# A two-part transformer block on one core: norms as two VectorE steps each, weight pieces split amid the masks, another opening

## The chip, the core and the metric

The kernel runs on one core of a Trainium2 chip. It is written engine by engine: TensorE (PE, with its weight loads PEld), VectorE (DVE), ScalarE (ACT), GpSimd (POOL) and the DMA queue of SyncE (SP) each run their own list of instructions in order, and wait for one another by semaphores. The metric is the device time of one execution in microseconds, the median of several runs.

## The reference

A modulation is computed from a small vector, then `x` (2 sequences of 2048 rows, 256 columns) goes through a stack of three linear-attention layers, gated and added to `x`, and then through two layers of local attention, gated and added again. The first stack, the "first half", is what the change touches.

```python
mod = (_silu(L0_c) @ L0_wmod).reshape(L0_c.shape[0], 6, 1, -1)
sa, ca, ga, sb, cb, gb = (mod[:, 0], mod[:, 1], mod[:, 2], mod[:, 3], mod[:, 4], mod[:, 5])
ga = (2 * (ga >= 0) - 1) * jnp.maximum(jnp.abs(ga), 0.25)
h = _layernorm(x, axis=-1) * (1 + ca) + sa
x = x + ga * _L0_attn_ref(h, ...)          # three layers, below
h = _layernorm(x, axis=-1) * (1 + cb) + sb
x = x + gb * _L0_ffn_ref(h, ...)           # two layers of local attention and an MLP
...
for l in range(L):                         # L = 3, 16 heads of 16
    q = (out @ Wq[l] + bq[l]).reshape(B, S, N_HEAD, dh)
    ...
    Qf = favor(q, omega[l])
    Kf = favor(k, omega[l])
    a = causal_linear_attention(Qf, Kf, v).reshape(B, S, D)
    a = a @ Wo[l] + bo[l]
    h = layer_norm(out + a, ln1_g[l], ln1_b[l])
    y = jax.nn.relu(h @ W1[l] + bf1[l]) @ W2[l] + bf2[l]
    out = layer_norm(h + y, ln2_g[l], ln2_b[l])
```

## The kernel before

The first half works in chunks of 512 rows (four tiles of 128): 8 chunks per layer, 24 in all. Every engine runs the same loop over `n`. Iteration `n` does the attention of chunk `n`, the output projection and first norm of chunk `w = n-1`, the MLP of chunk `m = n-2` (eight blocks `hb`: `up` on PE, `relu` on ACT, `rounded` on DVE, `down` on PE), and the second norm of chunk `z = n-3`. Operands of large products are split into a high half (`XTH`, `WH`, `RH`) and a low half (`XTL`, `WL`, `RL`), with three products for each; the low half is a subtraction, on DVE or on POOL. The order of an engine's work is written out by hand in the loops, so whatever stands behind a waiting instruction on its engine waits too.

PE in iteration `n`: `up` 0, `spread` (of the inverse denominators, tile `SPR`), `up` 1, `proj`, `down` 0, `proj`, `up` 2, `values`, `down` 1, `favor`, `up` 3, `favor`, `down` 2 (which needs RL of block 2 from POOL), `attn_out`, `key_sums` (needs ZC from POOL), `up` 4, `turn_k`, `down` 3, then four stages of `scores`, `up`, `down`, `sums`, where `sums` needs the masked scores U from DVE (`masks`); `down` 4 needs RL from POOL. In stage 3 the turned tiles of the next `proj` are made (`turn_x`), and DVE makes their low halves (`lower`, XTL).

A norm before is `statistics` on DVE, `rsqrt` on POOL, `normed` on DVE (line 1080, subtract the mean and multiply), then gain and bias on POOL: `gain1` and `bias1` for the first norm (1580, 1586), `second_norm` for the second (1605 to 1614; in the last layer also the gate and the sum with `x`, held in `PX`), `modulated` for the norm behind the stack (1622, 1624; chunks 16 to 23, `CH3`), `prologue` for the one ahead of it (1544, 1546; chunks 0 to 7, two iterations ahead of use). DVE's residual add `Z<-PS,X` (1240) waits for `second_norm` of two chunks earlier, whose tile it overwrites.

Weights come in 12 pieces per layer through two staging buffers `SG1`, so a piece may be loaded only when the piece before the last has been split. Pieces of layer 0 are all split ahead of the loop; those of layers 1 and 2 in iterations 7 to 10 and 15 to 18, three to five at a time behind the last masks or at the head of an iteration.

The opening loads constants and the modulation's weights (`wmod`, six DMAs), PE waits for all constants (`ZT` is the last) and makes 12 products into banks 0 to 5, DVE copies them, norms chunk 0 and computes the gates. The second half begins on every engine behind `first_half_over`.

## Time and profile before

| | us |
|---|---|
| median of 3 runs | 3425.41 (3416.5 to 3429.06) |
| profiled execution | 3431.8, of which span 3429.9 |
| busy PE / DVE / POOL / ACT | 2835.1 / 2123.1 / 1921.7 / 1441.5 |
| granted clock, mean | 0.918 |
| first half ends (last X) | about 1756 |

The page gives busy time by engine; windows cut it by stage; the list of waits says which engine's work ended another's idle time, and the timeline shows the instructions in order, each with the idle time before it in brackets. PE's two clock levels are 2.4 and 1.2 GHz; a granted clock of 0.96 over a stretch means that 8% of it ran at the lower level.

### The profile page before, as it was taken

How to read it: one execution, taken by the hardware profiler on the slowest of the kernel's cores; microseconds unless marked ns; L12 is line 12 of the kernel's file. 1: busy time of each engine (PE TensorE's matmuls, PEld its weight loads, DVE VectorE, ACT ScalarE, POOL GpSimd, SP SyncE). 2: the span in 40 equal slices, each digit the busy share in tenths (PEclk: the TensorE clock that was granted, in tenths of full speed). 3: DMA queues.
4: the chain of work that ended last, by engine and by line, in shares of the span. 5: the costliest groups of instructions: out<-in, count | busy, mean ns of one | idle time of the engine just before them, and what ended most of it. 6: DMA issues, size and time to landing. Idle time of an engine off the chain costs nothing. (4 is left out here: it accounts for less than half of the span.)

```text
span 3429.9 us, 61913 instructions
## 1 busy us (share of the span) xinstructions
PE 2835.1 (83%) x22184; PEld 2294.2 (67%) x22184; DVE 2123.1 (62%) x4931; ACT 1441.5 (42%) x3009; POOL 1921.7 (56%) x1732
## 2 busy tenths in 40 slices
PE   3698898989998988787627888898888889888886
PEld 1476776777776776676515677777667677767675
DVE  4556666665666665555435667666666766666664
ACT  1344344344353343333104554555545455545451
POOL 2356555555555556666655556555656655665653
PEclk7899999999999999999858899999999899999998
DMA  3000000010000010000020000000010100000000
GB/s 84 13 13 7 14 1 13 7 31 1 2 3 12 11 27 13 19 14 19 19 73 12 11 13 11 13 14 11 8 38 19 34 23 18 25 14 26 23 23 30
DMA packets 78001, 65.66 MB, mean 19 GB/s; under 512 B 15410, under 2 KB 72714, under 8 KB 77706
## 3 DMA queue, kind: packets, MB, share of 16 engines
q1 hardware_dynamic: 77706, 61.70, 6.1%
q8 instruction: 188, 3.08, 0.4%
q14 instruction: 107, 0.88, 0.1%
HBM read 49.10 MB, written 12.58 MB: 18 GB/s over the span
## 5 line engine op out<-in xcount | busy, mean ns | idle before, releaser
L967 ACT ACTIVATE PR<-PS,SM 128x256 f32<-128x256 f32 (+1 forms) x512 | 279.4, 554 | 444.3 <-DVE SM L1340 441.0
L858 ACT ACTIVATE FB<-PS,BC 128x512 f32<-128x512 f32 x192 | 132.1, 688 | 475.8 <-PE PS L250 475.2
L250 PE MATMUL PS<-WH,RH 128*128 128x256 f32 x768 | 230.9, 301 | 112.6 <-POOL RL L1566 110.2
L1728 POOL TENSOR_TENSOR OTL<-OO,OTH 128x512 fp32r<-128x512 f32 x64 | 82.4, 1288 | 359.0 <-ACT OTH L990 359.0
L250 PE MATMUL PS<-XTH,WH 128*128 128x512 f32 x576 | 251.7, 437 | 35.4 <-DVE XTL L1085 19.1
L1335 DVE CUSTOM_DVE_ANT_0 PS<-PS,MSK 128x256 f32<-128x256 f32 (+1 forms) x512 | 202.6, 436 | 116.1 <-PE PS L250 116.0
L1134 DVE TENSOR_TENSOR U<-PS,CST 128x512 f32<-128x512 f32 x384 | 238.2, 683 | 45.6 <-PE PS L250 45.5
L250 PEld LDWEIGHTS PS<-WH,RH 128*128 128x128 f32 x768 | 150.6, 196 | 154.7 <-issue 151.6
L1719 POOL TENSOR_TENSOR SM<-SM,COL 128x8 f32<-128x8 f32 x128 | 235.0, 1836 | 10.7
L250 PE MATMUL PS<-XTL,WH 128*128 128x512 f32 x576 | 232.9, 404 | 0.0
L250 PE MATMUL PS<-XTH,WL 128*128 128x512 f32 x576 | 231.9, 403 | 0.0
L250 PE MATMUL PS<-PT,VV 128*64 128x128 f32 x1984 | 143.6, 289 | 97.3 <-issue 76.6
L250 PE MATMUL PS<-WH,RL 128*128 128x256 f32 x768 | 223.3, 291 | 0.0
L250 PE MATMUL PS<-WL,RH 128*128 128x256 f32 x768 | 222.7, 290 | 0.0
L1566 POOL TENSOR_TENSOR RL<-FB,RH 128x512 fp32r<-128x512 f32 x96 | 142.7, 1486 | 134.4 <-DVE RH L1112 134.4
L866 ACT COPY NUM<-PS 128x256 f32<-128x256 f32 x96 | 35.7, 372 | 429.5 <-DVE TMP L1126 371.4
L250 PEld LDWEIGHTS PS<-PT,VV 128*64 128x64 f32 x1984 | 117.0, 144 | 117.4 <-issue 116.8
L250 PEld LDWEIGHTS PS<-XTH,WH 128*128 128x128 f32 x576 | 113.0, 196 | 109.5 <-issue 89.9
L250 PE MATMUL PS<-VH,XBH 128*128 128x512 f32 x384 | 179.8, 468 | 1.2 <-ACT SQ L939 1.2
L250 PE MATMUL PS<-KT,QT 64*128 64x256 f32 (+1 forms) x1024 | 175.8, 471 | 2.9 <-ACT RS L984 1.8
L1651 POOL TENSOR_TENSOR XTL<-NUM,XTH 128x512 fp32r<-128x512 f32 x48 | 79.0, 1669 | 167.9 <-ACT XTH L891 167.9
L250 PE MATMUL PS<-VL,XBH 128*128 128x512 f32 x384 | 162.6, 423 | 0.0
(212 smaller groups left out, 9165.0 us busy)
## 6 DMA issues: line engine op xcount, KB each, us to landing
PX<-in_L_attn_x SPq DMA_DIRECT2D x16, 512.0 KB, 3.9
TB<-in_k_rot SPq DMA_DIRECT2D x64, 128.0 KB, 2.1
SG<-in_L_attn_W SPq DMA_DIRECT2D x24, 256.0 KB, 2.8
...
```

The source lines that it names most:

```text
L250: return e.matmul(o, l, r, start=start, stop=True, skip_group_check=True)
L858: e.activation(FB[:, hb % 2, :], PS[:, 5, :], ACT.Relu, bias=BC[:, l % 2, 4 + hb:5 + hb]).then_inc(*a_re.up(n, hb))
L866: e.copy(NUM[:, :, 128 * j:128 * j + 128], PS[:, 4, 0:256].rearrange("p (m q) -> p m q", m=2)).then_inc(*a_nu.up(n, j))
L967: t = e.activation(PR[:, par, 256 * i + lo:256 * i + hi], PS[:, 3 + par, 256 * i + lo:256 * i + hi], ACT.Exp, bias=S[:, 40 + 2 * g + i:41 ...
L1134: e.tensor_tensor(heads(U[:, u % 6, :], 4), heads(PS[:, g, :], 4), bcast(CM, 4), ALU.mult).then_inc(*d_mk.up(n, u))
L1335: t = e.tensor_tensor_reduce(o, o, MSK[:, z:z + hi - lo], 1.0, NEG, ALU.add, ALU.max, S[:, 32 + 2 * g + i:33 + 2 * g + i])
L1566: e.tensor_tensor(RL[:, r, :], FB[:, 0, :], RH[:, r, :].bitcast(F), ALU.subtract).then_inc(*p_rl.up(n, hb))
L1651: e.tensor_tensor(XTL[:, 0, k, :], NUM[:, k, :], XTH[:, 0, k, :].bitcast(F), ALU.subtract).then_inc(*p_al.up(w, k))
L1719: e.tensor_tensor(o, a, MHALF.broadcast_to([128, 8]), ALU.pow).then_inc(*h_rs.up(u, i))
L1728: e.tensor_tensor(OTL[:, :], OO[:, :], OTH[:, :].bitcast(F), ALU.subtract).then_inc(*h_ol.up(u))
```

## The change

- Each norm of the first half becomes `statistics`, `centred` (subtract the mean, multiply by the gain) and `scaled` (multiply by the inverse deviation, add the bias): two groups of four DVE instructions of 128x256; `rsqrt` stays on POOL. POOL's `gain1`, `bias1`, `second_norm`, `modulated` and the wide operations of `prologue` are gone. For the last layer POOL multiplies gain and bias by the gate once (`gate_rows`) and adds the gated bias to `PX` per chunk (`add_bias`).
- On DVE the casts of block 2 and 4 (`rounded`) move ahead, `centred` of the first norm stands ahead of the denominators and the first masks. On POOL `low_hidden` 2 moves ahead of the XTL subtractions and 4 ahead of `rsqrt`; `add_bo` moves behind `rsqrt`.
- On PE `key_sums` moves from ahead of `up` 4 to behind `down` 3.
- `PLAN` says where each weight piece is split: one by one behind the masks of stages 0 to 2, at the head of an iteration or behind `values`; also for layer 0, from iteration 0 on.
- The opening loads the first columns of `wmod` ahead of the constants, makes two of the six modulation rows ahead of the wait for them, puts them into banks 4 to 7, 0 and 1, lets ACT copy five of them, and moves the gates into iteration 0.

```diff
+    PLAN = {(0, "v"): (3,), (0, "m0"): (4,), (0, "m1"): (5,), (0, "m2"): (6,), (1, "a"): (7, 8), (1, "v"): (9,), (1, "m0"): (10,), (1, "m1"): (11,)}
+    for b in (12, 24):
+        s = 8 * (b // 12)
+        PLAN |= {(s - 1, "m0"): (b,), (s - 1, "m1"): (b + 1,), (s - 1, "m2"): (b + 2,), (s, "m0"): (b + 3,), (s + 1, "m0"): (b + 4,),
+                 (s + 1, "m1"): (b + 5,), (s + 1, "m2"): (b + 6, b + 7), (s + 2, "a"): (b + 8, b + 9), (s + 2, "v"): (b + 10, b + 11)}
+
+    MODS = [(0, 0, 4), (1, 0, 5), (0, 1, 6), (1, 1, 7), (0, 2, 0), (1, 2, 1)]
...
-        e.wait_ge(*s_cst.at(4))
-        e.wait_ge(*s_wm.at(5))
         e.wait_ge(*d_cb.at(3))
-        for b in range(2):
-            for j in range(3):
-                for k in range(2):
-                    t = mm(e, PS[:, 3 * b + j, :], FB[:, 0, 128 * (2 * b + k):128 * (2 * b + k) + 128], FQ[:, k, j, :], k == 0)
-                t.then_inc(*e_mod.up(3 * b + j))
-        e.wait_ge(*d_mod.at(5))
+        e.wait_ge(*s_wm0.at(1))
+        for i, (b, j, bank) in enumerate(MODS):
+            if i == 2:
+                e.wait_ge(*s_wm.at(1))
+            for k in range(2):
+                t = mm(e, PS[:, bank, :], FB[:, 0, 128 * (2 * b + k):128 * (2 * b + k) + 128], FQ[:, k, j, :], k == 0)
+            t.then_inc(*e_mod.up(i))
+            if i == 1:
+                e.wait_ge(*s_cst.at(4))
...
-            if live:
-                if n > 0:
-                    e.wait_ge(*a_nu.at(n - 1, 3))
-                key_sums(n)
             if mlp:
                 up(m, 4)
             if live:
                     turn_k(n, i)
             if mlp:
                 down(m, 3)
+            if live:
+                if n > 0:
+                    e.wait_ge(*a_nu.at(n - 1, 3))
+                else:
+                    e.wait_ge(*d_mod.at(0))
+                key_sums(n)
             for j in range(4):
                 if live:
...
-        def normed(key, outs, tiles):
+        def centred(key, outs, tiles, gain):
             a = ST[:, NORM[key] % 4, :]
+            e.wait_ge(*d_ag.at(*key))
+            for j, (o, t) in enumerate(zip(outs, tiles)):
+                t = e.scalar_tensor_tensor(out=o, in0=t, scalar=a[:, 48 + 2 * j:49 + 2 * j], in1=gain, op0=ALU.subtract, op1=ALU.mult)
+            t.then_inc(*d_na.up(*key))
+
+        def scaled(key, outs, tiles, biases):
+            a = ST[:, NORM[key] % 4, :]
+            e.wait_ge(*d_na.at(*key))
             e.wait_ge(*p_rs.at(*key))
-            for j, (os, parts) in enumerate(zip(outs, tiles)):
-                for o, part in zip(os, parts):
-                    t = e.tensor_scalar(o, part, a[:, 48 + 2 * j:49 + 2 * j], a[:, 56 + j:57 + j], ALU.subtract, ALU.mult)
-            return t
+            for j, (o, t, b) in enumerate(zip(outs, tiles, biases)):
+                t = e.scalar_tensor_tensor(out=o, in0=t, scalar=a[:, 56 + j:57 + j], in1=b, op0=ALU.mult, op1=ALU.add)
+            t.then_inc(*d_nb.up(*key))
...
         prologue(0)
...
-        e.wait_ge(*d_gate.at(5))
-        e.tensor_copy(CT[:, 0:1], CT[:, 12:13]).then_inc(*d_mod.up(8))
-        for p in range(3):
-            split(p)
+        split(0)
+        split(1)
+        e.wait_ge(*e_mod.at(0))
+        e.tensor_copy(modulation(0, 0), PS[:, MODS[0][2], :]).then_inc(*d_mod.up(0))
+        e.wait_ge(*d_mod.at(0))
+        e.tensor_scalar(MOD[:, 0, D:2 * D], MOD[:, 0, D:2 * D], 1.0, None, ALU.add, ALU.bypass).then_inc(*d_mod.up(1))
+        e.wait_ge(*d_mod.at(1))
+        modulate_a(0)
+        modulate_b(0)
         for k in range(2):
             lower(0, k, 2 + k, 0, a_x, d_x)
+        e.memset(VP[:, :, :], 0.0).then_inc(*d_one.up())
+        split(2)
         prologue(1)
-        for p in range(3, 12):
-            split(p)
+        modulate_a(1)
+        modulate_b(1)
...
-            if n in (10, 18):
-                for p in range(12 * l + 8, 12 * l + 12):
-                    split(p)
+            splits(n, "a")
             if mlp:
                 rounded(m, 1)
             if two:
                 e.wait_ge(*d_y.at(z, 1))
                 statistics(("2", z), ztiles(z))
+                if z < 16:
+                    e.wait_ge(*s_row[4].at(z // 8))
+                else:
+                    e.wait_ge(*p_gr.at(1))
+                centred(("2", z), ztiles(z), ztiles(z), row(4) if z < 16 else MOD[:, (z % 8) // 4, D:2 * D])
+            if mlp:
+                rounded(m, 2)
             if live:
                 e.wait_ge(*d_one.at())
...
             if two:
-                normed(("2", z), ztiles(z), ztiles(z)).then_inc(*d_n2.up(z))
-            if mlp:
-                rounded(m, 2)
+                if z < 16:
+                    e.wait_ge(*s_row[5].at(z // 8))
+                    scaled(("2", z), xtiles(z), ztiles(z), [row(5)] * 4)
+                else:
+                    e.wait_ge(*p_pb.at(z))
+                    scaled(("2", z), ptiles(), ztiles(z), ptiles())
+            splits(n, "v")
...
-                        if w - 2 < 16:
-                            e.wait_ge(*p_out.at(w - 2, i))
-                        else:
-                            e.wait_ge(*p_fin.at(w - 2, i))
+                        e.wait_ge(*d_nb.at("2", w - 2))
                     e.tensor_tensor(pair(Z[:, w % 2, i, :]), pair(PS[:, 2 + i, :]), xpair(w, i), ALU.add).then_inc(*d_z.up(w, i))
+            if mlp:
+                rounded(m, 4)
+            if wo:
+                e.wait_ge(*d_z.at(w, 1))
+                statistics(("1", w), ztiles(w))
+                e.wait_ge(*s_row[2].at(w // 8))
+                centred(("1", w), ztiles(w), ztiles(w), row(2))
             if live:
                 e.wait_ge(*e_dd.at(n))
                 if wo:
...
+            if live:
+                masks(n, 0)
+            splits(n, "m0")
             if wo:
-                e.wait_ge(*d_z.at(w, 1))
-                statistics(("1", w), ztiles(w))
-            if mlp:
-                rounded(m, 4)
-            if live:
-                masks(n, 0)
-            if wo:
-                normed(("1", w), ztiles(w), ztiles(w)).then_inc(*d_n1.up(w))
+                e.wait_ge(*s_row[3].at(w // 8))
+                scaled(("1", w), ztiles(w), ztiles(w), [row(3)] * 4)
             if mlp:
                 rounded(m, 5)
...
             if mlp:
                 rounded(m, 7)
             if n + 2 < 8:
                 prologue(n + 2)
+                modulate_a(n + 2)
             if z in CH3:
-                c = z % 8
-                e.wait_ge(*p_fin.at(z, 1))
-                t = [[tile_of(PX, j)] for j in range(4)]
-                statistics(("3", z), t)
-                normed(("3", z), [[X[:, 4 * c + j, :]] for j in range(4)], t).then_inc(*d_n3.up(z))
+                e.wait_ge(*d_nb.at("2", z))
+                statistics(("3", z), ptiles())
+                centred(("3", z), xtiles(z), ptiles(), MOD[:, (z % 8) // 4, 4 * D:5 * D])
             if live:
                 state(n, 2)
                 masks(n, 3)
-            if n in (7, 15):
-                for p in range(12 * l + 12, 12 * l + 15):
-                    split(p)
-            if n in (8, 16):
-                split(12 * l + 3)
-            if n in (9, 17):
-                e.wait_ge(*e_dn.at(m, 3))
-                for p in range(12 * l + 4, 12 * l + 8):
-                    split(p)
...
             if live:
                 state(n, 3)
+            if n + 2 < 8:
+                modulate_b(n + 2)
+            if z in CH3:
+                scaled(("3", z), xtiles(z), xtiles(z), [MOD[:, (z % 8) // 4, 3 * D:4 * D]] * 4)
...
+        def gate_rows(b):
+            if b == 0:
+                e.wait_ge(*s_row[4].at(2))
+                e.wait_ge(*s_row[5].at(2))
...
+            e.tensor_tensor(MOD[:, b, D:2 * D], row(4), G, ALU.mult)
+            e.tensor_tensor(MOD[:, b, 0:D], row(5), G, ALU.mult).then_inc(*p_gr.up(b))
+
+        def add_bias(n):
+            e.wait_ge(*s_x.at("r", n))
+            e.wait_ge(*p_gr.at(b))
+            x = PX.rearrange("p i (t d) -> p (i t) d", t=2)
+            e.tensor_tensor(x, x, bcast(MOD[:, b, 0:D], 4), ALU.add).then_inc(*p_pb.up(n))
...
             if mlp:
                 low_hidden(m, 0)
-            if live:
-                add_bo(n)
-            if n in (10, 18):
-                for p in (12 * l + 9, 12 * l + 11):
-                    split(p)
+            splits(n, "a")
             if two:
                 rsqrt(("2", z))
+            if z in CH3:
+                add_bias(z)
+            if live:
+                add_bo(n)
+            if mlp:
+                low_hidden(m, 2)
...
-            if mlp:
-                low_hidden(m, 2)
+            splits(n, "v")
...
-            if two:
-                second_norm(z)
+            if mlp:
+                low_hidden(m, 4)
             if wo:
                 rsqrt(("1", w))
-            if mlp:
-                low_hidden(m, 4)
-            if wo:
-                gain1(w, 0)
-                bias1(w, 0)
+            splits(n, "m0")
             if live:
                 key_state(n, 0)
-            if wo:
-                gain1(w, 1)
+            splits(n, "m1")
             if mlp:
                 low_hidden(m, 6)
             if live:
                 key_state(n, 1)
-            if wo:
-                bias1(w, 1)
+            splits(n, "m2")
             if n + 2 < 8:
-                prologue(n + 2)
+                rsqrt(("p", n + 2))
             if z in CH3:
-                modulated(z)
+                rsqrt(("3", z))
...
         load_x(0)
         wm = ins["L0_wmod"].rearrange("(k p) n -> p k n", p=128)
         for k in range(2):
-            for j in range(3):
-                e.dma_start(FQ[:, k, j, :], wm[:, k, 512 * j:512 * j + 512]).then_inc(*s_wm.up(3 * k + j))
+            e.dma_start(FQ[:, k, 0, :], wm[:, k, 0:512]).then_inc(*s_wm0.up(k))
+        e.dma_start(CST[:, :, :], ins["k_cst"]).then_inc(*s_cst.up(0))
+        e.dma_start(COL[:, :], ins["k_col"]).then_inc(*s_cst.up(1))
+        load_piece(0)
+        load_piece(1)
+        for k in range(2):
+            e.dma_start(FQ[:, k, 1:3, :], wm[:, k, 512:1536].rearrange("p (j n) -> p j n", j=2)).then_inc(*s_wm.up(k))
...
-        load_piece(0)
-        load_piece(1)
...
-        for p in range(3, 12):
+        for p in (3, 4):
+            load_piece(p)
+        load_x(2)
+        for p in (5, 6, 7, 8):
+            load_piece(p)
+        load_x(3)
+        for p in (9, 10, 11):
...
```

DVE, iteration of a middle chunk, from the residual add of chunk `w` to the first block behind the masks; `ST` holds the statistics, `RD` the denominators, `U` the masked scores, `BB` the rows of gains and biases. Before:

```order
L1240 TENSOR_TENSOR Z<-PS,X 128x512 x2
L1245 TENSOR_SCALAR RD<-PS 128x128
L1247 RECIPROCAL RD<-RD 128x128
L1068 BN_STATS ST<-Z 128x6 x4
L1072 BN_AGGR ST<-ST 128x2 x4
L1112 CAST RH<-FB 128x512
L1134 TENSOR_TENSOR U<-PS,CST 128x512 x4
L1080 TENSOR_SCALAR Z<-Z,ST 128x256 x4
L1112 CAST RH<-FB 128x512
L1115 TENSOR_TENSOR RL<-FB,RH 128x512
```

and now:

```order
L1289 TENSOR_TENSOR Z<-PS,X 128x512 x2
L1158 CAST RH<-FB 128x512
L1091 BN_STATS ST<-Z 128x6 x4
L1095 BN_AGGR ST<-ST 128x2 x4
L1102 SCALAR_TENSOR_TENSOR Z<-Z,ST,BB 128x256 x4
L1301 TENSOR_SCALAR RD<-PS 128x128
L1303 RECIPROCAL RD<-RD 128x128
L1180 TENSOR_TENSOR U<-PS,CST 128x512 x4
L1110 SCALAR_TENSOR_TENSOR Z<-Z,ST,BB 128x256 x4
L1158 CAST RH<-FB 128x512
L1161 TENSOR_TENSOR RL<-FB,RH 128x512
```

The cast of block 4, the statistics and four new instructions stand ahead of the denominators and the masks, where the statistics stood behind the denominators.

POOL, from the second norm's `rsqrt` or the XTL subtractions of chunk `w` to the low half of block 4. Before:

```order
L1651 TENSOR_TENSOR XTL<-NUM,XTH 128x512 x2
L1566 TENSOR_TENSOR RL<-FB,RH 128x512
L1658 TENSOR_TENSOR ZC<-ZC,FQ 128x512 x2
L1605 TENSOR_TENSOR Z<-Z,BB 128x512
L1608 TENSOR_TENSOR X<-Z,BB 128x512
L1605 TENSOR_TENSOR Z<-Z,BB 128x512
L1608 TENSOR_TENSOR X<-Z,BB 128x512
L1528 TENSOR_SCALAR ST<-ST 128x4
L1530 TENSOR_TENSOR ST<-ST,COL 128x4
L1566 TENSOR_TENSOR RL<-FB,RH 128x512
```

and now:

```order
L1577 TENSOR_SCALAR ST<-ST 128x4
L1579 TENSOR_TENSOR ST<-ST,COL 128x4
L1605 TENSOR_TENSOR X<-X,BB 128x512 x2
L1610 TENSOR_TENSOR RL<-FB,RH 128x512
L1671 TENSOR_TENSOR XTL<-NUM,XTH 128x512 x2
L1677 TENSOR_TENSOR ZC<-ZC,FQ 128x512 x2
L1610 TENSOR_TENSOR RL<-FB,RH 128x512
```

The four operations of the second norm are gone from between ZC and the low half of block 4, and the low half of block 2 stands ahead of XTL.

SP, the first loads: `CST`, `COL`, `HSEL`, `SPR`, `ZT` are constants, `FQ` holds `wmod`, `SG` the weight pieces. Before:

```order
L1841 DMA CST<-in_k_cst 128x640
L1842 DMA COL<-in_k_col 128x5
L1813 DMA PX<-in_L_attn_x 128x4x256
L1847 DMA FQ<-in_L_wmod 128x512 x6
L1848 DMA HSEL<-in_k_hsel 128x64
L1849 DMA SPR<-in_k_spread 128x256
L1851 DMA ZT<-in_k_zero 1x1
L1837 DMA SG<-in_L_attn_Wq 128x2x256
L1837 DMA SG<-in_L_attn_Wk 128x2x256
```

and now:

```order
L1819 DMA PX<-in_L_attn_x 128x4x256
L1850 DMA FQ<-in_L_wmod 128x512 x2
L1851 DMA CST<-in_k_cst 128x640
L1852 DMA COL<-in_k_col 128x5
L1843 DMA SG<-in_L_attn_Wq 128x2x256
L1843 DMA SG<-in_L_attn_Wk 128x2x256
L1856 DMA FQ<-in_L_wmod 128x1024 x2
L1857 DMA HSEL<-in_k_hsel 128x64
L1858 DMA SPR<-in_k_spread 128x256
L1860 DMA ZT<-in_k_zero 1x1
```

Chunk 0 and a third of `wmod` stand ahead of the constants, and the first two weight pieces ahead of the rest of `wmod`.

## Rows read from the trace of the kernel before

**Rows 1.** Windows: us, busy us (x instructions) of PE, PEld, DVE, ACT, POOL, clock, DMA share, GB/s.

```profile
45.90:122.50 76.60, 40.08 (x316) 26.98 (x316) 36.23 (x68) 19.33 (x31) 27.09 (x19) 0.70 0.23 59
179.80:1269.70 1089.90, 973.71 (x8677) 793.12 (x8676) 701.08 (x1341) 455.01 (x748) 606.13 (x494) 0.96 0.04 11
825.10:886.70 61.60, 56.45 (x513) 46.05 (x512) 39.52 (x75) 26.71 (x44) 33.33 (x27) 0.97 0.00 1
1269.70:1635.00 365.30, 302.01 (x2541) 243.65 (x2541) 209.97 (x431) 132.58 (x218) 224.39 (x187) 0.92 0.05 15
1635.00:1719.70 84.70, 57.71 (x331) 49.54 (x330) 40.98 (x90) 13.11 (x20) 52.54 (x44) 0.88 0.06 19
```

**Rows 2.** Waits of PE, 179.8 to 1269.7: us in total, times, longest.

```profile
PE PS L250 <- POOL RL L1566: 74.6, 33, 3.0
PE PS L250 <- POOL WL L1535: 9.6, 2, 4.9
PE PS L250 <- DVE XTL L1085: 8.8, 2, 4.6
PE PS L394 <- DVE U L1134: 8.5, 4, 2.2
```

**Rows 3.** Timeline of PE, quiet iteration: start, us, instruction, [idle before <-releaser].

```profile
847.34 0.35 PE L250 MATMUL PS<-WH,RH 128*128 128x256 f32 x1 [1.84 <-POOL RL L1566]
...
862.15 0.36 PE L250 MATMUL PS<-WH,RH 128*128 128x256 f32 x1 [2.83 <-POOL RL L1566]
```

**Rows 4.** Timeline of DVE, quiet iteration, and one row from the last norm.

```profile
837.54 0.76 DVE L1212 TENSOR_TENSOR VP<-PS,BB 128x256 f32<-128x256 f32 x2 [4.93 <-PE PS L250]
...
841.07 0.43 DVE L1112 CAST RH<-FB 128x512 fp32r<-128x512 f32 x1 [0.21 <-ACT FB L858]
842.68 3.45 DVE L1226 TENSOR_TENSOR_SCAN ZC<-COL,FK 128x512 f32<-128x512 f32 x2 [1.19 <-ACT FK L847]
...
853.13 0.69 DVE L1240 TENSOR_TENSOR Z<-PS,X 128x512 f32<-128x512 f32 x1 [3.88 <-POOL X L1608]
...
857.54 1.34 DVE L1068 BATCH_NORM_STATS2 ST<-Z 128x6 f32<-128x256 f32 x4
...
859.52 2.48 DVE L1134 TENSOR_TENSOR U<-PS,CST 128x512 f32<-128x512 f32 x4
...
866.89 0.42 DVE L1126 TENSOR_TENSOR SBD<-PS,CST 128x256 f32<-128x256 f32 x1 [1.58 <-PE PS L250]
...
1749.45 1.38 DVE L1080 TENSOR_SCALAR X<-PX,ST 128x256 f32<-128x256 f32 x4 [1.42 <-POOL ST L1530]
```

**Rows 5.** Timeline of POOL, quiet iteration.

```profile
841.62 3.44 POOL L1651 TENSOR_TENSOR XTL<-NUM,XTH 128x512 fp32r<-128x512 f32 x2 [7.63 <-ACT XTH L891]
845.02 2.18 POOL L1566 TENSOR_TENSOR RL<-FB,RH 128x512 fp32r<-128x512 f32 x1
...
852.96 1.29 POOL L1605 TENSOR_TENSOR Z<-Z,BB 128x512 f32<-128x512 f32 x1
```

**Rows 6.** Timeline: a DVE instruction alone, then POOL and DVE side by side.

```profile
39.34 0.69 DVE L1170 SCALAR_TENSOR_TENSOR GB<-FB 128x512 f32<-128x512 f32 x1
...
715.27 2.57 POOL L1651 TENSOR_TENSOR XTL<-NUM,XTH 128x512 fp32r<-128x512 f32 x2
...
715.33 3.30 DVE L1080 TENSOR_SCALAR Z<-Z,ST 128x256 f32<-128x256 f32 x4
```

**Rows 7.** Waits of PE, 1269.7 to 1635.

```profile
PE PS L250 <- DVE Z L1240: 23.7, 5, 5.6
```

**Rows 8.** Timeline of PE in the opening.

```profile
12.54 12.46 PE L250 MATMUL PS<-FQ,FB 128*128 128x512 f32 x24 [12.54 <-DMA ZT<-in_k_zero]
...
83.10 1.98 PE L250 MATMUL PS<-U,OM 128*64 128x512 f32 x4 [21.90 <-DVE VP L1212]
```

**Rows 9.** Waits of PE, 1635 to 1758.

```profile
PE PS L596 <- POOL X L1624: 36.7, 1, 36.7
PE PS L250 <- POOL RL L1566: 21.3, 5, 6.4
```

204 lines of the change are left out of this document (84 added, 120 removed).

## The prediction, made before the changed kernel ran

> **What bounds the kernel now.** PE has by far the largest busy share on the page, so the time is PE's work plus PE's waits, and the other engines count only where PE waits for them. I then read windows that cut the first half at the points where PE spreads the denominators (one such point per iteration) [rows 1]. The reader should see three things there. A quiet iteration (825.1 to 886.7) lasts 61.6 us with PE busy 56.45 and a granted clock of 0.97. The 17 iterations from 179.8 to 1269.7 last 64.1 us each, and over them PE stands idle 116 us and loses about 4% (44 us) to the lower clock level. The five iterations in which the last layer's output is normed (1269.7 to 1635) last 73.1 us each. What is left of an iteration of the 17 without idle time and without low clock is (1089.9 - 116.2 - 43.6) / 17 = 54.7 us: PE's own work, which the change leaves alone.
>
> Next, who ends PE's waits. In the 17 iterations it is above all POOL with the low half of the hidden tile (RL), 74.6 us in 33 waits, then the split weights (WL, XTL) 18.4 us, and the masks U 8.5 us [rows 2]. The timeline of the quiet iteration shows the two RL waits, 1.84 and 2.83 us [rows 3]. DVE and POOL show why [rows 4, 5]: the first RL stands on POOL behind two XTL subtractions and then takes 2.18 us; the second stands behind the first norm's statistics, and these behind DVE's residual add (Z, line 1240), which waits 3.88 us for POOL's gain and bias of the second norm, work that PE does not need for another five iterations or more.
>
> **Norms (every iteration).** Removed from POOL: gain and bias of both norms, eight operations of some 1.29 us [rows 5], 10.3 us per iteration. Removed from DVE: eight TENSOR_SCALARs of 1.38 / 4 = 0.35 us [rows 4]. Added on DVE: sixteen SCALAR_TENSOR_TENSORs of 128x256. The trace has none of that shape. The nearest is 0.69 us for 128x512 alone [rows 6], so about 0.35 for half, the pitch of the TENSOR_SCALAR; from above, four DVE operations beside POOL's XTL took 3.30 us, 0.83 each [rows 6]; from below, half of the 0.43 that a cast of 128x512 takes [rows 4], 0.21. I take 0.35 where POOL is idle and 0.83 beside XTL. Net: DVE +2.8 us per iteration, and 2 more where scaled 2 meets XTL. Where these lie: *centred 2* in front of VP, where DVE now idles 4.93 us [rows 4], costs nothing; *scaled 2* beside XTL delays the scan, hence ZC, by 1.5 to 3.5 us, and it is for this that key_sums moves behind up(4), turn_k and down(3) on PE (4 us later), so it costs nothing if ZC is less than 4 us late; *centred 1* stands ahead of RD and the first masks, *scaled 1* where the four TENSOR_SCALARs stood.
>
> I walked one iteration with the durations of the rows, from the spread at 825.1. RL(2) now is ahead of XTL: ready at 842.9, PE wants it at 845.5: the 1.84 us go. XTL is ready at 846.4, PE wants it at 847.1. ZC is ready at 851 to 852, PE wants it at 853.8. Z no longer waits for POOL: 850.2 to 852.5. RL(4) is ahead of rsqrt: ready at 854.3, PE wants it at 857: the 2.83 us go. Then DVE is the tight one: statistics 1.8 [rows 4], centred 1 1.4, RD about 1.2, masks 2.5 [rows 4] end at 859.8, where PE wants the last of them at about 859: **a new wait of 0.8 us**, 2 us if centred 1 meets POOL's RL(4). From the second masks on, DVE has its present slack (1.58 us in front of the first state) [rows 4]. So 54.7 + 0.5 small waits + 1 for the masks + 1.3 of low clock = 57.5 us.
>
> By the Trainium skill (SBUF — State Buffer, "Who interferes with whom") a DVE instruction with two SBUF inputs contends with a GpSimd instruction that reads SBUF, and whichever started first holds the shared pair while the other blocks. Every new step has two such inputs, so this speaks against the change; the 3.30 us beside XTL agree in direction [rows 6]. If each step met a POOL operation, it would give rival D below.
>
> **Weight pieces.** DVE's casts (0.43) and every second subtraction (about 0.7) leave the place ahead of the XTL of the next proj, where they cost PE 18.4 / 4 = 4.6 us at four places [rows 2], and stand between masks. There DVE has 1 to 2 us of slack per stage, and the wait for the next DMA (a piece may be loaded only when the piece before the last is split) now passes beside 6 us of PE work. SP's queue keeps its order but for x loads, which are cheap to wait for. I charge 1 us in each of 8 iterations.
>
> **Iterations with a prologue (four of the 17).** Statistics 1.8, a wait of 1.42 for rsqrt and the norm's 1.38 in front of masks(3) [rows 4], 4.6 us, become 3.2; PE's four waits of 2.1 us for U [rows 2] and those for the state behind them shrink to about 1.5 together: 1.5 us above the quiet ones. The 17: 17 x 57.5 + 8 + 6 = 992 against 1089.9: **-98**.
>
> **The last layer's output (five iterations).** POOL loses eight operations of 1.28 for the second norm and four for the modulation, and gets one wide add (2 x 1.29 = 2.6 us) of the prepared bias. PE's wait for Z, 23.7 us in five [rows 7], goes, and so does much of the low clock (0.92) [rows 1]. DVE has 3.2 us more ahead of masks(3), as in a prologue: 60 us against 73.1: **-65**.
>
> **Opening.** PE waits to 12.54 us for ZT, the last of the constants, and computes the 12 products in 12.46 us [rows 8]; norm, modulation on POOL, gates and splits follow before the first proj at 45.9. Afterwards the first four products run while ZT is under way (ZT lands near 13, with 0.5 MB more ahead of it), the other eight take about 7 us, the pace at which the later ones of the 12 went, the norm and three splits are done beside them, and turn_x, cast and subtraction follow: first proj at about 24, **-22** (bounds -16 and -26: the clock may fall between the two groups, and the piece loads may delay ZT). Behind it the 21.9 us for VP go [rows 8], since nine pieces are no longer split ahead of it; some 6 us of low clock and prologue go too; the gates, moved into n = 0, add 4.5 us alone, partly beside ZC, and the pieces add 2: **-22** for 45.9 to 122.5. The next iteration (57.3 us) loses the wait for ZC and part of the prologue: **-3**.
>
> **End of the first half.** In n = 24 and 25 PE idles 27 of 84.7 us, mostly on RL behind POOL's norm work [rows 1, 9]: **-20**. Then PE waits 36.7 us for the last modulated X [rows 9]. Afterwards this chain is: POOL's add 2.6, Z 1.9, statistics 1.8, rsqrt 1.3, wide add 2.6, scaled 1.4, statistics 1.8, centred 1.4, scaled 1.4 = 16: **-20**. The second half itself is unchanged.
>
> **Sum.** -22 - 22 - 3 - 98 - 65 - 20 - 20 = -250. The profiled execution took 3431.8 us (span 3429.9), so 3182; against the median of the runs, 3425.4, it is 3175. I say 3185, because a walk like this misses small waits more often than it invents them.
>
> **The rivals.**
> *A, DVE becomes the bound.* If the port makes centred 1 and scaled 1 cost 0.83 each (6.6 us instead of 2.8), masks come 4 us later and each iteration lasts 61.5, the five 64: -44 - 3 - 44 - 45 - 40 = -176: **3255**. For it: DVE's busy time goes from 39.5 [rows 1] to 42 or more of 57, and its work there is serial. Against: POOL is nearly empty in just that stretch once gain and bias are gone.
> *B, key sums come late.* If scaled 2 and the scan beside XTL push ZC past PE's place for key_sums, RD, masks and sums all shift by 2 to 3 us in 22 iterations: +55: **3240**. For it: the scan already takes 3.45 / 2 = 1.73 beside POOL [rows 4], and ZC has 2 to 3 us to spare in my walk, no more.
> *C, no new wait at all.* 55.5 us per iteration and no low clock: **3135**.
> *D, slower than before.* All sixteen steps contended and all on the path: 16 x 0.83 - 8 x 0.34 = 10.6 us more per iteration, times 24 = 254, which eats the -250 and gives **3436**. It decides from about 10 us per iteration; centred 2 would have to outlast the 4.93 us in front of VP. The same mechanism, halfway, is the case of no change.
> *E, the opening gains half only* (products held up by loads, VP still waiting for a piece): **3204**, inside the forecast's own range.
>
> **How the numbers follow.** Forecast with E 0.57 (3160 to 3215), C 0.11, B 0.13, A 0.15, no change 0.02, D 0.02. Range 3130 to 3275: C below, A with its uncertainty above. A measurement of this kernel tells about 0.5% (17 us) from no change; faster by more than that 0.96, within it 0.02, slower 0.02.
>
> **What would show it.** Right: RL waits of PE nearly gone; DVE's Z without a wait for POOL; iterations of 56 to 59 us, alike in layers 0 to 2; granted clock 0.97 or more in the 17; first proj before 28 us; spread of n = 0 near 78; PE's wait at the change of halves near 16. Wrong: PE waiting for U in every iteration (A), for ZC (B), SCALAR_TENSOR_TENSOR of 0.8 us in the mean, or DVE waiting for DMA amid the masks.

## The result and the profile after

| | before | changed |
|---|---|---|
| median of 4 runs each | 3421.36 (3416.5 to 3429.06) | 3123.67 (3119.33 to 3130.74) |
| ratio | | 0.913, 95% interval 0.9102 to 0.9158 |
| span of the profiled execution | 3429.9 | 3129.0 |
| granted clock, mean | 0.918 | 0.948 |

The kernel is 298 us faster; I had forecast 3185 with a range from 3130, so the direction is right and the gain is under-estimated by a fifth. The windows answer to [rows 1]; columns as there, from 0 to the end of the program without a hole, and the quiet iteration (690.40 to 745.90) once more by itself:

```profile
0.00:22.10 22.10, 13.43 (x32) 5.98 (x32) 10.84 (x30) 5.52 (x11) 4.29 (x11) 1.00 0.70 183
22.10:72.60 50.50, 36.47 (x320) 24.30 (x320) 41.20 (x78) 19.25 (x31) 13.68 (x12) 0.86 0.19 58
72.60:127.30 54.70, 39.23 (x378) 28.81 (x374) 39.27 (x79) 21.80 (x37) 19.68 (x18) 0.94 0.10 25
127.30:1082.50 955.20, 940.18 (x8675) 765.30 (x8674) 736.63 (x1492) 454.32 (x748) 393.42 (x356) 1.00 0.04 13
690.40:745.90 55.50, 55.10 (x513) 44.88 (x512) 41.01 (x83) 26.76 (x44) 21.14 (x19) 1.00 0.01 1
1082.50:1364.70 282.20, 274.85 (x2544) 223.47 (x2544) 228.72 (x491) 132.80 (x218) 130.24 (x116) 1.00 0.06 20
1364.70:1436.10 71.40, 57.49 (x331) 49.20 (x330) 44.89 (x107) 13.12 (x20) 26.92 (x23) 0.88 0.07 23
1436.10:1455.90 19.80, 0.04 (x1) 0.07 (x2) 16.66 (x42) 0.00 (x0) 9.66 (x9) 0.63 0.16 53
1455.90:3129.00 1673.10, 1401.60 (x9920) 1139.79 (x9920) 1077.08 (x2864) 797.60 (x1951) 952.47 (x930) 0.92 0.07 22
```

Three things are to be seen. From 127.3 to 1364.7 the clock is 1.00 throughout, and PE is busy 1215 of 1237 us. In the 17 iterations POOL, 606 us busy before, is down to 393; DVE has risen by 36 us only. And an iteration of the last layer (282.2 / 5 = 56.4) is nearly a quiet one (55.5). Stage by stage:

| stage | before | changed | difference | forecast |
|---|---|---|---|---|
| to the first proj | 45.9 | 22.1 | -23.8 | -22 |
| to the spread of n = 0 | 76.6 | 50.5 | -26.1 | -22 |
| next iteration | 57.3 | 54.7 | -2.6 | -3 |
| 17 iterations | 1089.9 | 955.2 | -134.7 | -98 |
| five of the last layer's output | 365.3 | 282.2 | -83.1 | -65 |
| n = 24 and 25 | 84.7 | 71.4 | -13.3 | -20 |
| PE's wait at the change of halves | 36.7 | 19.8 | -16.9 | -20 |
| second half | 1673.5 | 1673.1 | -0.4 | 0 |

PE's waits in the 17 iterations, against [rows 2] (us in total, times, longest):

```profile
PE PS L402 <- DVE U L1180: 4.2, 4, 1.1
PE PS L246 <- ACT FB L869: 3.6, 17, 0.2
PE PS L246 <- DVE RL L1161: 3.5, 4, 1.5
PE PS L246 <- DVE U L1180: 1.5, 8, 0.2
PE PS L246 <- POOL XTL L1671: 0.3, 1, 0.3
```

The 74.6 us for RL from POOL and the 18.4 for WL and XTL are gone. What this list shows in their place is small: 3.5 us for RL from DVE, in iterations in which weight pieces are split. Gaps under 0.15 us are not in it, and "busy" counts them as work; at the masks they matter, see below. The timelines of DVE and POOL in the quiet iteration show why PE's waits for POOL are gone (start, us, instruction, idle before and who ended it), against [rows 4, 5, 6]:

```profile
697.06 1.67 DVE L1102 SCALAR_TENSOR_TENSOR Z<-Z,ST,BB 128x256 f32<-128x256 f32 x4
706.42 0.43 DVE L1158 CAST RH<-FB 128x512 fp32r<-128x512 f32 x1 [7.69 <-ACT FB L869]
706.76 1.41 DVE L1249 TENSOR_TENSOR VP<-PS,BB 128x256 f32<-128x256 f32 x4
708.09 3.71 DVE L1110 SCALAR_TENSOR_TENSOR X<-Z,ST,BB 128x256 f32<-128x256 f32 x4
711.73 2.33 DVE L1267 TENSOR_TENSOR_SCAN ZC<-COL,FK 128x512 f32<-128x512 f32 x2
...
716.21 1.27 DVE L1289 TENSOR_TENSOR Z<-PS,X 128x512 f32<-128x512 f32 x2
...
719.72 1.68 DVE L1102 SCALAR_TENSOR_TENSOR Z<-Z,ST,BB 128x256 f32<-128x256 f32 x4
...
722.50 2.42 DVE L1180 TENSOR_TENSOR U<-PS,CST 128x512 f32<-128x512 f32 x4
```

```profile
706.93 1.29 POOL L1610 TENSOR_TENSOR RL<-FB,RH 128x512 fp32r<-128x512 f32 x1 [5.81 <-DVE RH L1158]
708.18 2.95 POOL L1671 TENSOR_TENSOR XTL<-NUM,XTH 128x512 fp32r<-128x512 f32 x2
714.33 3.10 POOL L1677 TENSOR_TENSOR ZC<-ZC,FQ 128x512 f32<-128x512 f32 x2 [3.21 <-DVE CZ L1269]
717.97 1.29 POOL L1610 TENSOR_TENSOR RL<-FB,RH 128x512 fp32r<-128x512 f32 x1 [0.53 <-DVE RH L1158]
```

The residual add Z at 716.21 has no idle time ahead of it, where it had 3.88 us. The new 128x256 step costs 1.67 / 4 = 0.42 us alone (centred 2, centred 1, scaled 1) and 3.71 / 4 = 0.93 beside XTL (scaled 2); I had taken 0.35 and 0.83. The Trainium skill (SBUF — State Buffer, "Who interferes with whom") says that such a step with two SBUF inputs contends with a POOL instruction that reads SBUF; the trace agrees for scaled 2, and shows that the other twelve steps of this iteration meet nothing that slows them (1.66 to 1.68 us for each four). The 3.30 us of [rows 6] that the prediction set beside this rule were those of a TENSOR_SCALAR, which reads one tensor of SBUF, so they showed contention but not that of two inputs.

The masks were the tight place of the forecast. The list of waits has only 0.19 us for them in this iteration, beside 0.2 for FB. But PE takes the masks one by one, with gaps between that are too short for the list. Its 32 products with the first masks stretch over 1.94 us (724.02 to 725.96), where the 32 of the next stage, whose masks are ready, take 1.01 (730.92 to 731.93):

```profile
724.02 0.76 PE L246 MATMUL PS<-U,VP 128*32 128x128 f32 x6
724.97 1.06 PE L246 MATMUL PS<-U,VP 128*32 128x128 f32 x26 [0.19 <-DVE U L1180]
725.96 1.15 PE L246 MATMUL PS<-FQ,FK 32*128 32x256 f32 x16
...
730.92 1.08 PE L246 MATMUL PS<-U,VP 128*32 128x128 f32 x32
731.93 0.93 PE L246 MATMUL PS<-FQ,FK 32*128 32x256 f32 x12
```

So the masks cost 0.93 us here, as much as the last of them is late. Over the 17 iterations the products of the first stage take 0.71 us more than 1.01 in the mean (0.5 in most, 0.9 in four, 1.3 in two); in the kernel before it is 0.28.

### The profile page after: what moved, and what is told of

Read it like the earlier page. It is cut to its first block, busy times and chain, and to the rows that moved or that the text cites. A ratio compares the mean times of both kernels' runs of the same rounds, so it can differ in the third digit from the quotient of the medians.

```text
span 3129.0 us, 61903 instructions
## 1 busy us (share of the span) xinstructions
PE 2763.3 (88%) x22184; PEld 2236.9 (71%) x22184; DVE 2195.3 (70%) x5180; ACT 1444.4 (46%) x3016; POOL 1550.3 (50%) x1472
## 4 chain that ended last, share of the span: by engine, by line
PE 35%; DVE 6%; issue 5%; ACT 4%; POOL 2%; DMA 1%; SPq 0%; POOLq 0%; ACTq 0%; DVEq 0%
PE PS L246 29%; PE PS L678 3%; DVE ZS L1479 2%; ACT PR L987 2%; PE PS L726 1%; DVE ST L1089 1%; PE PS L640 1%; PE PS L647 1%; POOL ZS L1756 1%; DVE PS L1384 1%; POOL ZS L1758 1%; DVE SM L1364 1%; PE PS L607 1%; DVE SM L1389 0%; ACT SQ L959 0%
## 5 line engine op out<-in xcount | busy, mean ns | idle before, releaser
L1610 POOL TENSOR_TENSOR RL<-FB,RH 128x512 fp32r<-128x512 f32 x96 | 123.6, 1288 | 290.5 <-DVE RH L1158 290.5
L246 PE MATMUL PS<-XTH,WH 128*128 128x512 f32 x576 | 242.2, 420 | 12.6 <-ACT FB L869 5.8
L246 PE MATMUL PS<-WH,RH 128*128 128x256 f32 x768 | 224.0, 292 | 13.5 <-POOL RL L1610 6.8
L246 PE MATMUL PS<-WH,RL 128*128 128x256 f32 x768 | 216.6, 282 | 0.0
L1158 DVE CAST RH<-FB 128x512 fp32r<-128x512 f32 x192 | 83.9, 437 | 186.6 <-ACT FB L869 186.6
L1618 POOL TENSOR_TENSOR SBD<-SBD,TMP 128x256 f32<-128x256 f32 x84 | 62.9, 749 | 255.3 <-DVE TMP L1172 255.3
L246 PEld LDWEIGHTS PS<-XTH,WH 128*128 128x128 f32 x576 | 109.0, 189 | 79.3 <-issue 58.6
```

The costliest lines, as they stand in the source:

```text
L246: return e.matmul(o, l, r, start=start, stop=True, skip_group_check=True)
L1158: e.tensor_copy(RH[:, r, :], FB[:, hb % 2, :]).then_inc(*d_rh.up(n, hb))
L1610: e.tensor_tensor(RL[:, r, :], FB[:, 0, :], RH[:, r, :].bitcast(F), ALU.subtract).then_inc(*p_rl.up(n, hb))
L1618: e.tensor_tensor(SBD[:, (tile + 1) % 2, :, :], SBD[:, tile % 2, :, :], TMP[:, :, :], ALU.add).then_inc(*p_sd.up(n, j))
```

## The experiments

Each kernel ran beside the kernel before on the same chip; that one's median was 3420.12, 3419.83 and 3423.48 us in the three groups of runs. The table gives what the traces show between the spreads 1 and 18 (the 17 iterations) and 18 and 23 (the five). Waits are those over 0.3 us in which PE runs neither a matmul nor a weight load, so the short gaps between masks are not in them. Clock is the sum, over the records of the granted clock, of length times what is missing to 1; it counts the lower level during waits too, where it costs nothing. Each trace is of one execution, while the medians are of four or more.

| kernel | median, us | ratio, 95% interval | 17 iterations | waits | clock | the five |
|---|---|---|---|---|---|---|
| before | 3421.36 | 1 | 1089.8 | 109.0 | 44.4 | 365.3 |
| old norms, new order | 3402.61 | 0.9932 to 0.9969 | 1076.2 | 88.8 | 64.9 | 359.4 |
| the same, norm 1 new | 3410.99 | 0.994 to 0.9973 | 1084.3 | 93.7 | 61.4 | 359.6 |
| the same, norm 2 new | 3330.59 | 0.9688 to 0.974 | 994.8 | 33.1 | 17.1 | 365.3 |
| changed | 3123.67 | 0.9102 to 0.9158 | 955.1 | 7.6 | 0.0 | 282.2 |
| old order | 3172.28 | 0.9253 to 0.9295 | 980.8 | 36.7 | 1.7 | 292.9 |
| key sums old | 3212.07 | 0.9372 to 0.9403 | 1017.4 | 46.1 | 20.5 | 299.9 |
| 1.4 us of pad | 3154.94 | 0.9204 to 0.924 | 978.5 | 10.5 | 1.7 | 288.8 |
| 2.8 us of pad | 3202.69 | 0.9349 to 0.9386 | 1009.0 | 32.1 | 13.7 | 298.1 |
| splits old | 3145.39 | 0.9187 to 0.9216 | 974.2 | 23.4 | 8.5 | 282.2 |
| constants first | 3132.67 | 0.9128 to 0.9166 | 955.1 | 7.6 | 0.0 | 282.2 |
| changed, repeated | 3123.68 | 0.9123 to 0.9152 | | | | |
| own version 1 | 3122.87 | 0.9119 to 0.9148 | 956.8 | 5.2 | 0.0 | 284.6 |
| own version 2 | 3113.65 | 0.9069 to 0.9105 | 947.5 | 0.7 | 0.0 | 282.2 |

### Order or norms

From the kernel before, the order alone. Cut to block 2 and key sums; block 4's rounding moves ahead of RD, and POOL's order changes likewise (RL(2) ahead of XTL, RL(4) ahead of rsqrt):

```diff
+            if mlp:
+                rounded(m, 2)
             if live:
                 e.wait_ge(*d_one.at())
...
-            if mlp:
-                rounded(m, 2)
...
-                key_sums(n)
             if mlp:
                 up(m, 4)
...
+                key_sums(n)
```

> The kernel before with the new order alone: RL(2) ahead of XTL, RL(4) ahead of the first rsqrt, rounding of tile 2 ahead of VP and of tile 4 ahead of RD, key sums behind down(3); gains and biases of the norms stay on POOL, splits and opening stay old. The old wait for RL(2), 1.84 us per iteration, should go; the 3.88 us that DVE's residual add waits for POOL's second norm stay, and RL(4) stays behind that add. Theory 'order and norms both': -1.84 x 22 = -40 to -60 with its clock, 3360 to 3380. Theory 'the order is the lever': nearly all of the 218 us that the iterations gained, 3200 to 3230. Theory 'the norms are the lever': 3400 to 3421.

Measured 3402.6, -17.5 against 3420.1, as the last theory said. The wait for RL(2) did go; the one for RL(4) turned into this one. First PE's wait for the residual add, then DVE's wait ahead of that add:

```profile
843.78 2.09 PE L250 MATMUL PS<-FQ,FK 32*128 32x256 f32 x16 [3.68 <-DVE Z L1240]
```

```profile
840.39 0.69 DVE L1240 TENSOR_TENSOR Z<-PS,X 128x512 f32<-128x512 f32 x1 [3.87 <-POOL X L1608]
```

Scores now wait directly for the residual add, which waits for POOL's second norm; one wait of 3.68 us replaces two of 1.84 and 2.83, and the lower clock level beside it eats most of the difference (64.9 us of clock instead of 44.4).

The other way round, everything new but the order:

> The changed kernel (two-step norms on DVE, new splits, new opening) with the old order inside an iteration: RL(2) on POOL behind XTL and the rounding of tile 2 on DVE behind scaled 2, RL(4) behind the first rsqrt and its rounding behind statistics, centred 1 and RD, key sums ahead of up(4). By the rows of the changed kernel: RL(2) 1.6 us late, ZC 2.3 us late, RL(4) about 2 us late; waits that follow one another push each other out, so about 3 to 4.5 us per iteration. Theory 'the norms are the lever' (POOL emptied is what counts): +30 or less, 3150. Theory 'order and norms both': +72 to +108 of waits and with the lower clock level 30 to 40 more, 3200 to 3270, waits of PE for RL and ZC back.

Measured 3172.3, +48.6. That lies between the two theories (3150 or less, 3200 to 3270) and hits neither. In the quiet iteration only one wait came back, POOL's RL(2) behind XTL, 1.83 us; being 1.8 us late there, PE finds ZC, RL(4) and the masks ready (the products of the first stage take 1.01 us in all 17 iterations). So the norms (with the new opening and splits) are worth 248 us without the order and the order 49 with the norms, 17.5 without: what the order frees is taken by the next wait as long as POOL's second norm is there. 'The norms are the lever' comes out nearest.

### Which norm

Norm 1 new moves gain and bias into DVE's two steps at the places where the changed kernel has them (statistics and centred 1 ahead of RD); norm 2 new does so for layers 0 and 1:

```diff
                 statistics(("2", z), ztiles(z))
+                if z < 16:
+                    centred(("2", z), d_c2, fztiles(z), fztiles(z), row(4))
...
-            if two:
+            if z in CH3:
                 second_norm(z)
```

> The run with the old norms in the new order (3402.6), with the first norm alone in the new form: centred 1 and scaled 1 on DVE, its gains and biases (four of POOL's eight operations) gone; the second norm keeps its TENSOR_SCALARs and POOL's four operations, old splits and opening stay. Asked: which norm carries the gain of the iterations. Theory Z (the chain through DVE's residual add is what cost: it waits for POOL's second norm, and RL(4) and all of DVE's late work stand behind it): the first norm alone gives little, the wait stays, 3380 to 3400. Rival E (both norms count alike, since what matters is POOL's total load): half of the some 180 us that the norms brought in the iterations, 3310 to 3330.

> The same kernel (old norms, new order, 3402.6) with the second norm alone in the new form, in layers 0 and 1 (16 of the 24 x chunks); the first norm and the last layer's output norm stay old. Theory Z: DVE's residual add no longer waits, so the 3.4 to 3.8 us of waits and 3.4 us of low clock per iteration go in the 15 iterations n = 4 to 18 whose second norm is of those layers: 7 x 15 = -100, 3300 (3285 to 3320), and iterations of 55.5 to 57 there. Rival E: half of the share of these iterations, 3340 to 3360.

Norm 1 alone: 3411.0, no gain over 3402.6 (the intervals of the two ratios overlap); DVE's wait for POOL's X is still 3.87 us. Norm 2 alone: 3330.6, -72, and the quiet iteration is that of the changed kernel but for 0.3 us. Norm 1 is still old there, so its new form is worth no more than these 0.3 us in a quiet iteration. The windows, of old norms, norm 1 new, norm 2 new:

```profile
811.00:872.20 61.20, 57.30 (x513) 46.88 (x512) 39.24 (x75) 26.72 (x44) 31.50 (x27) 0.94 0.01 1
```

```profile
814.60:875.60 61.00, 57.10 (x509) 46.52 (x508) 40.18 (x79) 26.72 (x44) 26.07 (x23) 0.94 0.00 1
```

```profile
825.90:881.70 55.80, 55.34 (x513) 45.23 (x512) 41.42 (x79) 26.66 (x44) 27.62 (x24) 1.00 0.01 1
```

POOL's busy time falls by 5.4 us in the second and by only 3.9 in the third; the time falls in the third alone. So it isn't POOL's load, rival E; it is the four operations that stand between ZC and the residual add, theory Z. The waits show this, and not the times: both lie outside the ranges of both theories (3380 to 3400 and 3310 to 3330 for norm 1, 3285 to 3320 and 3340 to 3360 for norm 2). The -100 expected came out at -81 in the 17 iterations (1076.2 to 994.8), since 5.4 us go per quiet iteration, not 7, and the four split places keep waits of 4.2 to 4.8 us; the last layer's five iterations gave 6 us back. Of the 83 us that the changed kernel gains in those five, no run tells the share of its norms by itself; in the norm 2 kernel, whose last layer is old, PE still waits 45.8 us for the residual add there, in five waits.

### Key sums

```diff
+            if live:
+                key_sums(n)
             if mlp:
                 up(m, 4)
```

> The changed kernel with one thing put back: PE's key sums stand again ahead of up(4), turn_k and down(3). In the changed kernel PE comes to key_sums at 718.93 in the quiet iteration, the three blocks take 3.78 us, and POOL is done with ZC at 717.44, so PE would ask 2.3 us too early, in some 21 iterations. Theory Q (a PE wait costs its own length and no more): +2.3 x 21 = 48, median 3172, granted clock stays 1.00 in the iterations. Theory P (waits of 2 us and more drag the lower clock level behind them, as the kernel before lost 44 us of clock beside 116 us of waits, 0.38 per us): +48 and +18, 3190, clock about 0.97. Theory N (the place of the key sums doesn't matter, since PE waits for the scores' inputs anyway): 3124 to 3130.

Measured +88, more than undoing the whole order (+49), and more than either theory. PE waits for ZC as computed (2.2 to 2.3 us, but 4.7 and 4.9 in two iterations with weight pieces), and two things come on top. In the trace of this kernel, first PE in one iteration, then DVE in another, whose clock is 1.00:

```profile
755.68 0.90 PE L246 MATMUL PS<-ZC,HSEL 128*32 128x128 f32 x16 [2.21 <-POOL ZC L1677]
756.51 0.80 PE L246 MATMUL PS<-XTH,WH 128*128 128x512 f32 x1
757.10 0.63 PE L246 MATMUL PS<-XTL,WH 128*128 128x512 f32 x1
757.53 0.63 PE L246 MATMUL PS<-XTH,WL 128*128 128x512 f32 x1
```

```profile
937.82 0.43 DVE L1158 CAST RH<-FB 128x512 fp32r<-128x512 f32 x1 [3.06 <-ACT FB L869]
938.16 1.40 DVE L1091 BATCH_NORM_STATS2 ST<-Z 128x6 f32<-128x256 f32 x4
```

The matmuls behind the wait take 0.43 us each from start to start, against 0.23 of the same rows in other iterations: the lower level, 3.4 us of it, 1.7 us lost each time, in 14 of the 22 iterations (in one of the two with the longest waits, twice as much). And the rounding of tile 4 now stands ahead of the statistics on DVE; with up(4) late, DVE stands idle 3.06 us, with its statistics, centred 1 and masks queued behind, and PE waits for the masks more than before: its first 32 products with them take 2.07 us there, and 1.55 in the same iteration of the changed kernel. Without low clock such an iteration lasts 58.5 us instead of 55.5. The two moves belong together: the early rounding is only free because key sums have left the place ahead of up(4).

### A wait of chosen size

```diff
             if live:
+                for i in range(4):
+                    e.bn_stats(SM[:, i % 4, 8 * (i // 4):8 * (i // 4) + 6], BB[:, 2, :])
                 masks(n, 0)
```

> The changed kernel with four more bn_stats of 128x256 (0.35 us each, 1.4 us) on DVE ahead of the first masks of each of the 24 iterations; they write to a scratch place that nothing reads. It measures the term of the prediction that was to cost 1 us (masks 0.8 us late) and turned out at 0.19. Theory Q: the masks are just in time, so 1.4 of pad cost 1.2 to 1.4 each, +32, median 3155, clock 1.00. Theory P: such waits bring the lower clock level too, +13 more, 3168, clock 0.98. Theory S (DVE has slack that the walk didn't see): under +10, 3130.

> As the run with four more bn_stats ahead of the first masks, which came out at +31 with masks 1.3 us later per iteration and no low clock, but with eight of them, 2.8 us. Theory Q: +2.7 x 24 = +65, 3189, clock 1.00. Theory P (longer waits bring the lower level, as where PE waited 2.3 us for ZC and then 0.5 for masks): half of the iterations lose 1.7 us more, +20, 3209. The masks' dribble (PE starts again with each tile) could keep the clock up where one wait of the same length doesn't.

1.4 us of pad: +31.3, which is 23.4 / 17 = 1.38 per iteration, all of the pad, and hardly any low clock. 2.8 us: +79, of which 53.9 in the 17 iterations. Quiet ones with the clock at 1.00 last 2.5 to 2.6 us longer, about 44 for 17; most of the rest are eight iterations with a stretch at the lower level, 1.7 us each. So the masks had no slack at all, as the walk said. Theory Q holds for the short wait; the longer one comes nearer to P (3209) than to Q (3189). The quiet iterations of both, 1.4 us of pad first:

```profile
764.10:820.90 56.80, 56.01 (x515) 45.41 (x515) 42.38 (x87) 26.72 (x44) 21.86 (x20) 1.00 0.01 1
```

```profile
786.00:844.00 58.00, 55.92 (x513) 45.38 (x512) 43.70 (x91) 26.72 (x44) 21.84 (x20) 1.00 0.00 1
```

### Weight pieces and opening

> The changed kernel with the weight pieces of layers 1 and 2 in the old groups (three behind masks(3), one, four behind masks(3), four ahead of the rounding of tile 1); everything else new. The new places cost 0.6 us in six iterations and 2.5 us in two, 8.6 together, by the iterations' lengths. Theory 'the old groups cost PE 4.6 us each at four places, as the waits of before for WL and XTL say' : +18 - 8.6, 3134 (3128 to 3142 with low clock behind such waits, 2 us each). Rival 'their cost was the crowded POOL of before, so they are as cheap now': 3115 to 3124.

+21.7 against the changed kernel beside it, 3 us above the first theory's range. The waits of before are back, 18.4 us together [rows 2], although POOL has some 200 us less to do; it isn't the crowded POOL but the place ahead of the next proj. Four iterations last 60.1 to 61.6 us, and 8.5 us of clock come with them:

```profile
PE PS L246 <- POOL WL L1584: 9.4, 2, 4.8
PE PS L246 <- DVE XTL L1114: 9.0, 2, 4.7
```

> The changed kernel, but PE waits for the last of the constants (12.9 us) before the first of the twelve products of the opening, as before, instead of before the third pair. In the changed kernel the first four products start at 7.5. Theory (the products are the opening's chain): first proj at 27 instead of 22.1, so +5, 3129. Rival (norm 0 and ACT's copies set it, the products wait in their shade): +1 to +2, 3125.

+9. The twelve products start at 13.14 instead of 7.52 and the first proj at 28.18 instead of 22.14: 6 us, the chain that the first theory names; the first spread comes 4.8 us later (77.4). Where the rest of the +9 lies isn't told: two traces of the changed kernel itself differ by 6.6 us (span 3129.0, and 3122.4 in the repeated one), 5.1 of it ahead of the second half. The rest of the opening's 50 us, above all the 21.9 us for VP that are gone, has no run of its own.

### Two versions of my own

> The changed kernel as it stands, run beside the others as their measure: 3124, 3119 to 3131.

It gave 3123.68 (3122.16 to 3124.85).

Version 1 puts scaled 2, the prologues and two late pieces each of layers 1 and 2 into DVE's 7.7 us idle stretch ahead of VP. It loads the BF constants of the second half during the first and the tables earlier, issues some of the scale loads from ACT, and puts POOL's wide add ahead of rsqrt:

> A version meant to beat the changed kernel, built on its trace. Four edits: (1) scaled 2 goes ahead of VP, into the 7.7 us in which DVE idles there, away from POOL's XTL (3.7 us beside it, 1.67 alone); (2) for n = 1 to 5 the whole prologue (statistics, centred, rsqrt, scaled) goes into the same idle stretch instead of standing ahead of masks(3), where PE waits 1.05 us for it; (3) pieces b+10 and b+11 go there too, where two iterations are 2.5 us longer; (4) at the change of halves the eight BF loads go into the first half's queue, the tables are loaded first, and half of the scale loads is issued by ACT (PE waits 15.1 us there); POOL's wide add goes ahead of rsqrt. Theory: prologues -5, split places -5, change of halves -7, wide add -1.3 to -2.2, so about -19: median 3105 (3095 to 3115). Rival (the idle stretch is too short: 6.8 us of new steps behind centred 2 push the rounding of tile 2 and VP back): no gain or slower, 3120 to 3150, with PE waits for RL or VP in the prologue iterations.

3122.87: the rival held, though not by the mechanism that it named. In the quiet iteration scan and XTL now run side by side, POOL first, then DVE:

```profile
705.55 4.36 POOL L1685 TENSOR_TENSOR XTL<-NUM,XTH 128x512 fp32r<-128x512 f32 x2
```

```profile
705.46 3.36 DVE L1279 TENSOR_TENSOR_SCAN ZC<-COL,FK 128x512 f32<-128x512 f32 x2
708.86 1.08 DVE L1281 COPY CZ<-ZC 128x2 f32<-128x2 f32 x1
```

XTL takes 4.36 us instead of 2.95, PE comes to attn_out 0.4 us late, and the iteration lasts 55.9. In three prologue iterations a wait of 1.56 us for XTL replaced that of 1.05 for the masks. That ate the gains elsewhere. scaled 2 beside XTL, which looks bad in the changed kernel (3.71 us), is what keeps the scan out of XTL's way, where it would cost PE time.

Version 2 takes scaled 2 back, and of the prologue moves statistics and centred only; the rest of version 1 stays:

```diff
                 centred(("2", z), ...)
+            splits(n, "i")
+            if 1 <= n < 6:
+                prologue(n + 2)
+                modulate_a(n + 2)
             if mlp:
                 rounded(m, 2)
```

> A second version meant to beat the changed kernel: scaled 2 is back behind VP (ahead of VP it let the scan run beside POOL's XTL, which took 4.36 us instead of 2.95 and made each quiet iteration 0.45 us longer). Kept: the pieces b+10 and b+11 in DVE's idle stretch, the loads at the change of halves (5.5 us earlier there), the wide add ahead of rsqrt. Of the prologue only statistics and centred move into the idle stretch; scaled stays at the iteration's end. Theory: -5 (two split places), -4 (four prologues), -5.5 (change of halves), -1: 3108 (3103 to 3113). Rival: given back again by a new collision, 3118 to 3124.

3113.65 (3109.36 to 3114.76), 10 us below the changed kernel; its interval (0.9069 to 0.9105) lies clear of the repeated one's (0.9123 to 0.9152). It beats both kernels, by a little less than expected (3103 to 3113). 7.6 us in the 17 iterations are there, and the last chain of the first half takes 17.6 us instead of 19.8, with the wide add ahead of rsqrt. But at the change of halves 7 us less of waiting for XBL turned partly into a new wait for POOL's split. The changed kernel's second wait there, and version 2's:

```profile
1471.60 0.66 PE L607 MATMUL PS<-CST,X 128*128 128x128 f32 x2 [15.08 <-DVE XBL L1351]
```

```profile
1452.98 0.66 PE L620 MATMUL PS<-CST,X 128*128 128x128 f32 x2 [8.14 <-DVE XBL L1373]
1460.69 0.77 PE L259 MATMUL PS<-VH,XBH 128*128 128x512 f32 x1 [4.47 <-POOL VL L1606]
```

## Why the prediction was right in direction and short in size

**The walk.** Set against the spread at the start of the iteration, its times were right within 0.6 us, but for the lower end of those for ZC (1.1):

| | walk: ready, wanted | trace: ready, wanted |
|---|---|---|
| RL(2) | 17.8, 20.4 | 17.8, 20.4 |
| XTL | 21.3, 22.0 | 20.7, 21.9 |
| ZC | 25.9 to 26.9, 28.7 | 27.0, 28.5 |
| Z done | 27.4 | 27.1 |
| RL(4) | 29.2, 31.9 | 28.9, 31.7 |
| last mask | 34.7, 33.9 | 34.5, 33.6 |

**What failed is what was added to it, the low clock above all.** 17 x (57.5 - 55.5) = 34 of the 37 us that the 17 iterations gained beyond the forecast are three terms. *Low clock, 1.3 per iteration:* measured 0, two thirds of the error. In the trace of the kernel before, all 32 stretches at the lower level between spreads 1 and 23 begin during a wait of PE of 1.8 us or more or within 1.4 us behind one; I let the waits go and kept a part of their clock. *Masks, 1 us:* measured 0.7 in the mean, so nearly right; the last mask was 0.9 us late, walked at 0.8, and the pad shows that the place had no slack. *Small waits 0.5:* 0.2 is left, for FB. What remains of 55.5, 54.6, is PE's own work, put at 54.7. The same three terms and DVE's 3.2 us ahead of masks(3), put at 2.5 and costing 1.05 of wait, make the five iterations of the last layer 56.4 and not 60: 18 us more. With the opening's 6 us and against the 10 us too much at the end of the half (both below) that is 51 us below the sum of 3175, and the step from 3175 to 3185 makes it 61.

**Norms.** Right, and for the reason given: the residual add's wait for POOL. I hadn't said that half of the norm change (norm 1) brings nothing by itself. The prices 0.35 and 0.83 were too low (0.42 and 0.93), without consequence where DVE had been idle.

**Weight pieces.** Right in the sum: 8 us charged, about 7.4 measured (four iterations 0.6 us longer, two 2.5). **Prologues:** 6 charged, 4.9 measured.

**Opening.** 24 forecast for the first proj, 22.1 measured; spread at 78, came at 72.6. Right, 6 us short in all.

**End of the half.** Over-estimated by 10 us. In n = 24 and 25 the waits for RL are smaller but not gone (between 1082.5 and 1436.1 there are 6.8 us for POOL's and 2.6 for DVE's). The last chain is 19.8 us, not 16: POOL's wide add stands behind rsqrt there, and DVE waits 2.2 us for it.

**The rivals.** C's 55.5 us per iteration and full clock are what happened, though not without a new wait: PE loses 0.7 us at the masks in every iteration. Its 0.11 was too little. That low clock came with waits could have been read from the trace before, and wasn't used. A and B did not happen. PE does wait for U in every iteration, the sign named for A, but centred 1 and scaled 1 cost 0.42 us a step and not 0.83, since POOL has only the short rsqrt beside them; and ZC had 1.5 us to spare. A's sum also left out the 14 us for pieces and prologues; with them it is 3269. D is excluded. The low end, 3130, had room for C's iterations but not for the opening's further 6 us, so the result, 3123.67, fell 6 us below the range. And the step from 3175 to 3185, because a walk misses small waits, was wrong here.
